# Blocks of 32 tokens and a transpose on VectorE for x of batches 2 to 7

## The reference

```
x = x + (x @ B0[id].T) @ A0[id].T                     # rank 16, one adapter per batch
base   = x @ W.T                                      # 2048 x 2048
logits = x @ Wr.T + 5 * onehot(language)              # 8 experts
gates  = softmax over the two largest logits
x = x + base + 2 * sum_e gates[e] * (x @ A[e].T) @ B[e].T
```

## Time and profile before

| | us |
|---|---|
| three runs | 1665.24, 1665.28, 1666.73 (median 1665.28) |
| profiled execution | 1665.4 |
| its span | 1663.6 |
| PE busy | 1629.2 (98%) |
| DVE busy | 1120.7 (67%) |
| ACT busy | 813.6 (49%) |
| mean granted clock of PE | 0.997 |

### The profile page before, as it was taken

The page is one execution under the profiler, slowest core; times in us unless marked ns, Lnnn a source line. Parts: engine busy times, 40 slices in busy tenths (PEclk is TensorE's granted clock), DMA queues, the critical chain, the costliest instruction groups (busy, mean ns, idle before and its releaser), DMA issues.

```text
span 1663.6 us, 21252 instructions
## 1 busy us (share of the span) xinstructions
PE 1629.2 (98%) x8128; PEld 1370.7 (82%) x8128; DVE 1120.7 (67%) x1503; ACT 813.6 (49%) x1096; POOL 9.8 (1%) x19
## 2 busy tenths in 40 slices
PE   7799999999999999999999999999999999999998
PEld 5677888888888888888888888888888888888887
DVE  3675344776587666876577765877568765877665
ACT  5544443255544654455544655446544555445443
POOL 1100000000000000000000000000000000000000
PEclk9899999999999999999999999999999999999999
DMA  8689897866567664776557665676647765566664
GB/s 246 187 222 247 212 242 200 229 203 208 176 219 240 210 204 164 252 219 215 187 190 253 209 204 175 235 236 204 208 167 245 222 213 186 192 225 216 203 217 162
DMA packets 201143, 351.27 MB, mean 211 GB/s; under 512 B 42394, under 2 KB 115402, under 8 KB 200010
## 3 DMA queue, kind: packets, MB, share of 16 engines
q1 hardware_dynamic: 198866, 345.72, 66.2%
q10 hardware_dynamic: 2176, 4.19, 0.9%
HBM read 280.62 MB, written 68.82 MB: 210 GB/s over the span
## 4 chain that ended last, share of the span: by engine, by line
PE 93%; DMA 2%; DVE 2%; ACT 2%; SPq 1%; issue 1%; ACTq 0%; DVEq 0%
PE pb L714 26%; PE pb L713 26%; PE pb L712 26%; PE pb L332 4%; PE pb L334 3%; PE pb L280 3%; PE pb L480 2%; PE pb L615 1%; DMA wrn<-in_L_cond_Wr_dram 0%; DMA raw<-in_L_cond_W_dram 0%; SPq L591 0%; DMA t_scr<-tst 0%; ACT xah L308 0%; DMA t_scr<-raw 0%; DMA bt_scr<-bt 0%
## 5 line engine op out<-in xcount | busy, mean ns | idle before, releaser
L708 DVE TENSOR_TENSOR wl<-raw,wh 128x1024 fp32r<-128x1024 f32 (+1 forms) x456 | 556.2, 1220 | 424.3 <-ACT wh L704 423.3
L704 ACT CAST wh<-raw 128x1024 fp32r<-128x1024 f32 (+1 forms) x456 | 476.9, 1046 | 695.3 <-PE pb L714 695.2
L712 PE MATMUL pb<-wh,sh 128*128 128x512 f32 x1568 | 617.9, 394 | 0.5 <-DVE ost L748 0.5
L714 PE MATMUL pb<-wh,sl 128*128 128x512 f32 x1568 | 613.3, 391 | 0.0
L713 PE MATMUL pb<-wl,sh 128*128 128x512 f32 x1568 | 612.4, 391 | 0.0
L714 PEld LDWEIGHTS pb<-wh,sl 128*128 128x128 f32 x1568 | 294.3, 188 | 63.0
L712 PEld LDWEIGHTS pb<-wh,sh 128*128 128x128 f32 x1568 | 294.7, 188 | 54.7 <-DVE wl L708 0.9
L713 PEld LDWEIGHTS pb<-wl,sh 128*128 128x128 f32 x1568 | 294.9, 188 | 53.8
L332 PE MATMUL pb<-awb,xah 128*128 128x304 f32 x512 | 140.8, 309 | 2.7 <-DVE aux L347 1.6
L334 PE MATMUL pb<-awb,xal 128*128 128x256 f32 x512 | 134.3, 280 | 0.0
L712 PE MATMUL pb<-wh,xh 128*128 128x512 f32 x256 | 105.3, 411 | 1.2 <-DVE ost L748 0.8
(11 more groups left out here) (134 smaller groups left out, 1340.6 us busy)
## 6 DMA issues: line engine op xcount, KB each, us to landing
raw<-t_scr SPq DMA_DIRECT2D x392, 512.0 KB, 3.7
xst<-in_x_dram SPq DMA_DIRECT2D x56, 512.0 KB, 4.8
raw<-in_L_cond_W_dram SPq DMA_DIRECT2D x128, 128.0 KB, 3.8
t_scr<-tst SPq DMA_DIRECT2D x32, 512.0 KB, 4.6
raw<-bt_scr SPq DMA_DIRECT2D x28, 512.0 KB, 3.6
out_dram<-ost SPq DMA_DIRECT2D x28, 512.0 KB, 3.4
out_dram<-u SPq DMA_DIRECT2D x28, 512.0 KB, 3.4
t_scr<-raw SPq DMA_DIRECT2D x32, 256.0 KB, 4.0
```

The costliest lines, as they stand in the source:

```text
L704: e.copy(pair_split(wh, g), pair_source(g)).then_inc(c_wh, 1)
L708: e.tensor_tensor(out=pair_split(wl, g), in0=pair_source(g), in1=pair_split(wh, g).bitcast(f32), op=ALU.subtract).then_inc(c_wl, 1)
L712: e.matmul(o, h, wh[:, g % RING, k, :], start=start, stop=False)
L714: return e.matmul(o, l, wh[:, g % RING, k, :], start=False, stop=stop)
```

## The change

For batches 2 to 7 (n >= 2), `x_load` issues 16 DMAs in place of one. They bring the same 512 KB, but each takes 32 partitions and runs of 32 elements (128 B), so that a partition holds token j of every block of 32 tokens, and a group of 32 partitions holds 32 of each 128 columns. The buffer's semaphore counts 256 for a load. DVE then transposes squares of 32 x 32 straight into the quarter of x (`x_turn`, one instruction of 128 x 512 a unit). PE's `x_transpose` and ACT's `x_keep` go for these batches; `x_turn` stands at the head of DVE's slot, ahead of `pair_lo`. Batches 0 and 1 stay as they are.

```diff
+        x_b = x.rearrange("b (h v j) (c k a i) -> b h c k a j v i", h=2, j=32, c=4, k=4, a=4)
+
+        def x_block(m):
+            return xst[:, m % 2, :, :].rearrange("p t n -> p (t n)").rearrange("p (v k i) -> p v k i", v=8, k=4)
+
+        def x_turn(e, n, u):
+            q, kp = x_unit(u)
+            m = u // 2
+            if u % 2 == 0:
+                e.wait_ge(d_x[m % 2], 64 + 256 * (4 * (n - 2) + m // 2 + 1))
+            if kp == 0:
+                b = n - 1
+                if q < 2:
+                    if n == 2:
+                        wait_used(e, SLOTS0 - 1)
+                    else:
+                        e.wait_ge(c_spl, split_of(b - 1, 6, 3) + 1)
+                else:
+                    e.wait_ge(c_spl, split_of(b, q, 3) + 1)
+                    e.wait_ge(c_add, 8 * b)
+            e.transpose(two(n, q, kp).rearrange("p (k v j) -> p v k j", k=2, v=8),
+                        x_block(m)[:, :, u % 2 * 2:u % 2 * 2 + 2, :]).then_inc(c_xc, 1)
+
         def x_load(e, n, m):
             half, cols = m // 4, m % 4
...
-            else:
+            elif n == 1 or (n == 2 and m < 2):
                 e.wait_ge(c_tr, 16 * n + 2 * m - 2)
-            e.dma_start(x_place(n, m), x_v[n, half, :, :, cols * CW:(cols + 1) * CW])\
-             .then_inc(d_x[m % 2] if n else d_x0[m % 4], 16)
+            else:
+                e.wait_ge(c_xc, 16 * n + 2 * m - 2)
+            if n < 2:
+                e.dma_start(x_place(n, m), x_v[n, half, :, :, cols * CW:(cols + 1) * CW])\
+                 .then_inc(d_x[m % 2] if n else d_x0[m % 4], 16)
+            else:
+                for a in range(4):
+                    for k in range(4):
+                        e.dma_start(x_block(m)[32 * a:32 * a + 32, :, k, :], x_b[n, half, cols, k, a])\
+                         .then_inc(d_x[m % 2], 16)
...
-                        if i in X_AT:
-                            x_transpose(e, n, X_AT[i])
...
-                            x_keep(e, n, X_AT[i])
                             x_hi(e, n, X_AT[i])
...
+                    if n < NB and i in X_AT:
+                        x_turn(e, n, X_AT[i])
                     if pair_of(b, i) + 2 < LAST:
                         pair_lo(e, pair_of(b, i) + 2)
```

More of the change, by code:

```diff
@@ L246, in x_load @@
                 e.wait_ge(c_bt, 4)
-            else:
-                e.wait_ge(c_tr, 16 * n + 2 * m - 2)
-            e.dma_start(x_place(n, m), x_v[n, half, :, :, cols * CW:(cols + 1) * CW])\
-             .then_inc(d_x[m % 2] if n else d_x0[m % 4], 16)
+            elif n == 1 or (n == 2 and m < 2):
+                e.wait_ge(c_tr, 16 * n + 2 * m - 2)
+            else:
+                e.wait_ge(c_xc, 16 * n + 2 * m - 2)
[7 more added lines that the diff above has]
+                         .then_inc(d_x[m % 2], 16)
         def x_unit(u):
```

## The result

| | before | after |
|---|---|---|
| median, us | 1665.24 (5 runs, 1664.58 to 1666.73) | 1674.7 (5 runs, 1673.48 to 1679.77) |
| span of the profiled execution | 1663.6 | 1672.7 |
| mean granted clock of PE | 0.997 | 0.988 |

The ratio is 1.0063, with an interval of 1.0046 to 1.0080: the kernel became slower by 0.6%, where 1626 us had been forecast, and it lies 3 us above the stated range.

What follows compares the result with a forecast made beforehand. The prediction took PE to bound the kernel: 1665.4 - 42.2 (transposes removed) + 3 (stalls from slow issues) = 1626.2, forecast 1626 us; likeliest case 1621 to 1634, 8-in-10 range 1618 to 1672.

Steps and rivals of the forecast that it cites:

- What bounds, and what goes: PE bounds batches 1 to 6; removing 16 L280 units saves 7.04 us a period, 42.2 us over six.
- DVE: Transpose at 0.68 us a unit, 10.9 us a batch, costing 0, or 1 us a batch at 1.2 us.
- The transfer: 4096 packets of 128 B a load: the rings can carry it, 3 to 6 us hiding beside 8.2 us of issue.
- up to 15 us of DMA time a load: Load time if each 32 KB piece held the rings nearly the skill's 0.95 us; the trace showed no such price.
- I take 8.2: On SP, 16 issues of an x load at 0.51 us each: 8.2 us, bounds 5.1 to 11.8.
- The places: Tight spots on SP: slots 45 and 48, where PE just does not wait, and slot 7, margin 0.7 us.
- (a): Slots 45 and 48: slot 55's piece leaves 6.9 us late; every further us of block is about 2 us later.
- 0.5 us of stall a batch: Allowance for the occasional slow issue on SP, 3 us in all.
- Rival 2: Issues at 0.56 us, block 9 us, 3 to 5 us of stall a batch: 1645 to 1655; chance 0.18.
- Rival 5: No change, stalls of 6 to 8 us a batch eating the gain: 1662 to 1669; chance 0.04.
- rival 3: SP becomes the bound at 0.74 us an issue, some 17 us of stall a batch: 1719; chance 0.19.
- The first stage: Two more loads go out at slots 28 and 30; cost 0, up to 3 us.

Runs made afterwards that it cites:

- one_dma: The changed kernel with each x load of batches 2 to 7 again one DMA of 2 KB runs, x in a wrong order: 1622.79 us.
- spread: The changed kernel with a load's 16 issues divided over several of SP's slots, W's pieces going out between them: 1632.54 us.
- long_runs: The changed kernel with 16 DMAs of 32 KB a load but runs of 1 KB, not 128 B, x in a wrong order: 1632.43 us.
- double_turn: The kernel with one DMA a load, every DVE transpose made twice, the first time into a scratch tile: 1630.49 us.

## Why the prediction was wrong

**What bounds, and what goes: right.** PE set the pace, and taking L280 off it was worth 7.24 us a period (predicted 7.04), shown by one_dma: 1622.8 us against 1665.4 - 42.2 = 1623.2.

**DVE: right.** The transpose of 128 x 512 takes 0.704 us, against 0.68 taken:

```profile
L262 DVE STREAM_TRANSPOSE pool_a<-xst x56: 701/704/712, 403.7 to 1418.5; 128x512 f32<-128x512 f32 x56
```

It costs PE nothing as it is, and doubled it cost 1.2 us a period, where 1 was predicted for a transpose of 1.2 us. The Trainium skill's page "VectorE: DVE Perf Modes", section "The three transpose paths", gives 311 ns for 128 x 128 in bf16; the 1.24 us for four of them was an estimate from that figure, and here one float32 instruction over the same 512 columns takes 0.704.

**The transfer: right in its conclusion.** A period's DMA busy time rose from 124 to 0.75 x 194.2 = 146 us, inside the 135 to 159 given, and the pieces land in 2.4 us. The rule of the Trainium skill that spoke against the change ("DMA: Bandwidth & Descriptors", section "Bandwidth", transfers under 64 KB are descriptor-dominated) does not decide: spread has the same 32 KB transfers and is faster than before by 2.1%. Nor did the pieces cost the up to 15 us of DMA time a load that the prediction had weighed: they added (146 - 124) / 8 = 2.7 us. (It said that the trace before has only larger transfers; there are two of 68 KB and three of 8.5 KB among them, which decide nothing.)

**The step that failed: "I take 8.2", the block of 16 issues.** It was sized from issues with long runs, and its upper end (11.8) was read as needing full rings. Long runs do give 8.09, and with them PE hardly waits in the six periods (0.5 us); the 128 B runs gave 9.57 on average, 12.07 at most. The places and the mechanism were right, and so was the remark that each further microsecond at (a) counts twice; but the margin was next to nothing, so 1.4 us decided the sign. Instead of the 0.5 us of stall a batch, there were 193.53 - 186.07 = 7.5 us, 44.7 us over six periods. Rival 2 had a block of 9 us and 3 to 5 us of stall; its mechanism came true with a longer block. Rival 5 had this outcome for the batches, stalls of 6 to 8 us that eat the gain, at a chance of 0.04; the first stage's loss then put the time above its 1662 to 1669. (In rival 3 the parts named sum to 3 x 3.5 + 3 + 6 = 19.5 us a batch and not 17; the forecast does not use them.)

**A term that was not there: the clock after a pause.** Fifteen pauses of PE after 350 us sum to 30.6 us in the trace; the six periods lost 44.7. A mean granted clock of 0.9912 over their 1161.15 us is 10.2 us more, all of it at 1.2 GHz behind six of the pauses. The last 4 us are not followed one by one. An estimate for more than half of them: matmuls start 0.23 us apart but are recorded 0.39 us long, so a pause costs some 0.16 us more than the idle time shown, 2.4 us in fifteen.

**The first stage: cost taken as 0 to 3 us, measured 7.1** (348.43 against one_dma's 341.37), by 4.92 of pause and the slow matmuls after it. The slots there last 6 to 7 us, but SP issues seven or eight DMAs in each already, and the load of W behind the block was needed two slots later. Unlike the stalls of the batches, this does not need short runs: long_runs lost 9.6 us there.

The sum, from one_dma: 1622.8 + 44.7 (six periods) + 7.1 (first stage) = 1674.6, measured 1674.7.

## What to carry to other kernels

An issuing queue is an engine with an order: when one DMA becomes sixteen, work out what stands behind the block on that queue and when the next engine wants it, with the spread of the issue times and not their best value. If the margin is near zero, forecast a coin's throw; past it, a pause of the bounding engine can cost more than its own length (here 44.7 us lost for 30.6 us of pauses). The remedy is cheap: issue such a block from a queue on which nobody waits (here GpSimd, 2.6% faster than before), or put the urgent DMAs between its parts.

## What the runs showed of the hardware

- DMAs of 32 KB issued back to back from SP took 0.45 us each with starts 0.49 apart; single ones took up to 2.25 us, and short runs made a block of 16 longer: 8.09 us for 1 KB runs, 9.57 for 128 B, where the eighth issue took 1.13 us on average (0.44 with 1 KB runs).
- The same DMAs took 0.582 us each on GpSimd, none over 0.72, and the profile counted 184,000 fewer packets for them.
- After a pause of 2.71 us PE's matmuls of 512 columns started 0.43 us apart, not 0.23, for most of the next 3.9 us; after one of 2.58 us the clock stayed full. After twelve pauses of 0.44 to 0.56 us (double_turn) the mean clock of the execution was 0.997, as before.
- A DVE transpose of 128 x 512 float32, in squares of 32 x 32, took 0.704 us.
